# Two-layer gated cross-attention block on one core: weighted sums of three key blocks in a row, 12 probability buffers, and a new step for most other work

## What is computed

```python
x = x + tanh(g_xattn[0]) * attention(layernorm(x), ctx)        # 16 heads of 16 channels
x = x + tanh(g_ffn[0])   * ternary_linear(layernorm(x))        # scale: a maximum over all of x
x = x + tanh(g_xattn[1]) * depool(layernorm(x), ctx, lengths)
x = x + tanh(g_ffn[1])   * int8_linear(layernorm(x))
# attention, for each batch and head:
k = concat(ctx_k, k); v = concat(ctx_v, v)                      # 120 + 256 = 376 keys
out = softmax(q * scale @ k.T) @ v                              # then @ w_proj.T + b_proj
```

## Time and profile before

| | before |
|---|---|
| median of 3 runs | 1188.46 us (1187.54 to 1188.80) |
| profiled execution | 1188.27 us, span 1186.5 us |
| busy share of the span | PE 93%, DVE 79%, ACT 70%, POOL 59% |
| granted TensorE clock, mean | 0.97 of full speed |
| attention stage | about 65 to 967 us of the span |
| row stage | about 975 us to the end |

### The profile page before, as it was taken

The page is one execution under the profiler, slowest core; times in us unless marked ns, Lnnn a source line. Parts: engine busy times, 40 slices in busy tenths (PEclk is TensorE's granted clock), DMA queues, the critical chain, the costliest instruction groups (busy, mean ns, idle before and its releaser), DMA issues.

```text
span 1186.5 us, 33451 instructions
## 1 busy us (share of the span) xinstructions
PE 1106.6 (93%) x8458; PEld 679.4 (57%) x8458; DVE 935.8 (79%) x2328; ACT 833.3 (70%) x1730; POOL 699.4 (59%) x1259
## 2 busy tenths in 40 slices
PE   3599999999999999999999999999999968988885
PEld 3255555555555555555555555555555537767673
DVE  4867777777777777777777777777777736999997
ACT  2157777777777777777777777777777747878874
POOL 4545666655555556655566665666664217777776
PEclk9699999999999999999999999999999977999997
DMA  4333343333333333333333333333333101222222
GB/s 135 96 83 105 103 105 105 97 100 102 101 101 101 101 105 96 97 101 99 96 98 101 101 102 100 103 103 106 88 94 86 40 26 35 69 86 86 86 87 88
DMA packets 158680, 110.18 MB, mean 93 GB/s; under 512 B 17154, under 2 KB 154788, under 8 KB 158628
## 3 DMA queue, kind: packets, MB, share of 16 engines
q1 hardware_dynamic: 156900, 108.78, 33.9%
q10 hardware_dynamic: 1728, 0.79, 0.2%
HBM read 30.30 MB, written 16.29 MB: 39 GB/s over the span
## 4 chain that ended last, share of the span: by engine, by line
PE 78%; DVE 10%; issue 4%; POOL 4%; DMA 1%; ACT 1%; DVEq 1%; POOLq 0%; SPq 0%; ACTq 0%
PE pv_ps L622 18%; PE ms_ps L607 16%; PE st_ps L597 15%; PE misc L645 9%; PE misc L648 5%; PE misc L653 5%; PE aux L669 2%; PE misc L637 1%; PE aux L674 1%; PE aux L663 1%; DVE am L1176 1%; DVE xs L1165 1%; DVE v L1159 1%; POOL xs L1035 1%; PE st_ps L1104 1%
## 5 line engine op out<-in xcount | busy, mean ns | idle before, releaser
L790 DVE TENSOR_REDUCE neg<-ms_ps 128x1 f32<-128x376 f32 x1024 | 528.7, 544 | 185.8 <-PE ms_ps L607 173.9
L887 ACT ACTIVATE probs<-st_ps 128x512 f32<-128x512 f32 x768 | 449.7, 601 | 156.8 <-PE st_ps L597 83.3
L607 PE MATMUL ms_ps<-k,q 96*128 96x376 bf16 x1024 | 335.0, 328 | 7.1 <-DVE neg L790 6.6
L597 PE MATMUL st_ps<-q,k 99*128 99x256 bf16 x1536 | 295.6, 274 | 0.7 <-ACT probs L887 0.6
L622 PE MATMUL pv_ps<-probs,v 128*32 128x256 f32 (+1 forms) x3072 | 245.4, 391 | 0.5 <-ACT oT L903 0.2
L597 PEld LDWEIGHTS st_ps<-q,k 99*128 99x128 bf16 x1536 | 134.4, 98 | 90.9 <-ACT probs L887 29.1
L607 PEld LDWEIGHTS ms_ps<-k,q 96*128 96x128 bf16 x1024 | 98.7, 96 | 128.5 <-DVE neg L790 115.4
L645 PE MATMUL misc<-xnT,wqkvT 128*128 128x256 f32 x512 | 155.1, 387 | 2.3 <-ACT xnT L916 1.5
L622 PEld LDWEIGHTS pv_ps<-probs,v 128*32 128x32 f32 (+1 forms) x3072 | 60.5, 108 | 117.5 <-issue 87.9
L468 POOL TENSOR_SCALAR negp<-neg 128x16 bf16<-128x16 f32 x64 | 13.0, 204 | 175.4 <-DVE neg L790 175.0
L485 POOL TENSOR_SCALAR parts<-qk 128x632 bf16<-128x632 f32 x64 | 46.0, 719 | 99.9 <-ACT qk L953 99.7
(11 more groups left out here) (186 smaller groups left out, 1821.2 us busy)
## 6 DMA issues: line engine op xcount, KB each, us to landing
k<-parts SPq DMA_DIRECT2D x384, 94.0 KB, 2.7
q<-parts SPq DMA_DIRECT2D x384, 64.0 KB, 2.4
xs<-in_x SPq DMA_DIRECT2D x32, 256.0 KB, 2.8
out_dram<-xn SPq DMA_DIRECT2D x32, 256.0 KB, 2.2
cx<-in_ctx SPq DMA_DIRECT2D x32, 240.0 KB, 2.8
recurrence_input<-u_in SPq DMA_DIRECT2D x32, 120.0 KB, 1.9
plug<-plugs SPq DMA_DIRECT2D x32, 120.0 KB, 3.2
powers<-gath SPq DMA_DIRECT2D x32, 120.0 KB, 1.9
```

The source lines that it names most:

```text
L597: mm = pe.matmul(st_ps[u % SR][:, j * S:(j + 1) * S], k6[0:KM, r, h, k * P:(k + 1) * P], q6[0:KM, r, h, :], start=True, stop=True)
L607: pe.matmul(ms_ps[t][:, 0:KEYS], q6[0:KR, r, h % HU, t * P:(t + 1) * P], k6[0:KR, r, h % HU, 0:KEYS], start=True, stop=True).then_inc(s_ms, 1)
L790: dve.tensor_reduce(neg[:, m, t, h % HU:h % HU + 1], ms_ps[t][:, 0:KEYS], AX.X, ALU.max, negate=True).then_inc(s_red, 1)
L887: act.activation(probs[:, u % PR, :], st_ps[u % SR][:, :], ACT.Exp).then_inc(s_exp, 1)
```

## The change

- `PR` goes from 8 to 12 buffers `probs`. At steps 1, 7, 13 and 19 PE now calls `attend` three times in a row, for the three key blocks of one head group; no other step has one.
- `negT` has a half for each of `neg0` and `neg1`. ACT only copies; the DMAs of the maxima rows are started by SP, `neg1`'s first in the body and `neg0`'s between the load of `cx` and the stack of half 1.
- The jobs and what ACT and DVE do get new steps (table `AT`): PE's `k`, `proj` and `v` one step later, `xT` at step 1, `o0` at 9; ACT's `xn` at 12 and 14, `decay` at 12, `vcx` at 14, `neg0` at 20 (21 before), `xnT` at 0; DVE's `norm` at 4, 10, 16 and 22, `mn` at 7, `mx` at 8, `update` at 18, `gath` at 21, `aggr1` at 23; and the second score blocks of a step move from steps 1 and 3 to steps 2 and 4 of each six.

The diff, cut to its core:

```diff
-    PR = 8
+    PR = 12
-        negT = sb("negT", [3 * HU, S], BF16)
+        negT = sb("negT", [3 * HU, 2, S], BF16)
         JOBS = {
-            "xT": (0, 0, 1, 2), "q": (0, 2, 4, 2), "k": (0, 7, 4, 2), "proj": (0, 13, 4, -1), "v": (0, 19, 4, 1),
-            "kcT": (1, 2, 1, 2), "o3": (1, 4, 1, -1), "aT": (1, 6, 1, -1), "neg1": (1, 8, 1, 0), "o0": (1, 10, 1, 0),
+            "xT": (0, 1, 1, 2), "q": (0, 2, 4, 2), "k": (0, 8, 4, 2), "proj": (0, 14, 4, -1), "v": (0, 20, 4, 1),
+            "kcT": (1, 2, 1, 2), "o3": (1, 4, 1, -1), "aT": (1, 6, 1, -1), "neg1": (1, 8, 1, 0), "o0": (1, 9, 1, 0),
             "o1": (1, 16, 1, 0), "neg0": (1, 20, 1, 1), "o2": (1, 22, 1, 0),
         }
+        AT = {
+            "cxp": 0, "xnT": 0, "copy_o": 2, "kc": 4, "csq": 4, "q": 6, "aT": 6, "neg1": 8, "xn": 12, "k": 11, "decay": 12,
+            "vcx": 14, "neg0": 20, "v": 23,
+            "stats0": 1, "aggr0": 2, "norm": 4, "update": 18, "stats1": 19, "aggr1": 23, "mx": 8, "mn": 7, "gath": 21,
+        }
-            counts = [1, 2, 1, 2, 1, 1] * NG
+            counts = [1, 1, 2, 1, 2, 1] * NG
...
                 b, opp = i * 2 + par, 1 - par
+                if live(b):
+                    own_wait_taken(sp, b, "neg1")
+                    sp.dma_start(q6[KR:KM, 2 * par + 1, :, :], negT[:, 1, :]).then_inc(d_neg[2 * par + 1], 16)
...
                     sp.dma_start(cx[0:NP, opp, :], ctx_2048[b + 3]).then_inc(d_cx[opp], 16)
+                if live(b + 1):
+                    own_wait_taken(sp, b, "neg0")
+                    sp.dma_start(q6[KR:KM, 2 * opp, :, :], negT[:, 0, :]).then_inc(d_neg[2 * opp], 16)
                 if live(b + 2):
                     stack(b + 2, par, 1)
...
                     if u == 1 and live(b - 1):
-                        attend(b - 1, opp, NG * NKT - 1)
-                    elif u % 2 and u > 1 and live(b):
-                        attend(b, par, (u - 3) // 2)
+                        for k in range(NKT):
+                            attend(b - 1, opp, (NG - 1) * NKT + k)
+                    elif u % (2 * NKT) == 1 and u > 1 and live(b):
+                        for k in range(NKT):
+                            attend(b, par, (u // (2 * NKT) - 1) * NKT + k)
...
-                def neg_rows(B, pB, m, waits):
+                def neg_rows(B, iB, pB, m):
                     wait_full(act, b, f"neg{m}")
-                    if waits:
-                        act.wait_ge(d_neg[2 * par + 1 - m], i * 16 + 16)
-                    act.copy(negT[:, :], aux[:, :].bitcast(BF16)[0:3 * HU, 0:S]).then_inc(s_free[1], 1)
-                    own_wait_taken(act, b, f"neg{m}")
-                    act.dma_start(q6[KR:KM, 2 * pB + m, :, :], negT[:, :]).then_inc(d_neg[2 * pB + m], 16)
+                    if live(B - 1):
+                        act.wait_ge(d_neg[2 * (1 - pB) + m], (iB + (pB - 1) // 2) * 16 + 16)
+                    act.copy(negT[:, m, :], aux[:, :].bitcast(BF16)[0:3 * HU, 0:S]).then_inc(s_free[1], 1)
```

More of the change, by code:

```diff
@@ L812, in body @@
                     maxima([first])
-                    if u == 1 and live(b + 3):
+                    if u == AT["stats0"] and live(b + 3):
                         dve.wait_ge(d_x[opp], (i + (par + 3) // 2) * 16 + 16)
@@ L819, in body @@
                             dve.bn_stats(bn[:, t, :], xs[:, b + 3, t, :]).then_inc(s_stat0, 1)
-                    if u == 4 and live(b + 3):
+                    if u == AT["aggr0"] and live(b + 3):
                         own_wait(dve, s_stat0, (b + 3) * 4 + 2)
@@ L823, in body @@
                             dve.bn_aggr(mv0[:, t, :], bn[:, t, :]).then_inc(s_stat0, 1)
-                    if u == 5 and live(b - 1):
+                    if u == AT["norm"] and live(b - 1):
                         normalise(b - 1, 3)
-                    if u in (10, 16, 22) and live(b):
-                        normalise(b, (u - 10) // 6)
-                    if u == 17 and live(b - 1):
+                    if u > AT["norm"] and u % 6 == AT["norm"] % 6 and live(b):
+                        normalise(b, (u - AT["norm"]) // 6 - 1)
+                    if u == AT["update"] and live(b - 1):
                         wait_full(dve, b, "proj")
@@ L833, in body @@
                                                  xs[:, b - 1, :, :], ALU.mult, ALU.add).then_inc(s_free[0], 1)
-                    if u == 19 and live(b - 1):
+                    if u == AT["stats1"] and live(b - 1):
                         own_wait_taken(dve, b, "proj")
@@ L837, in body @@
                             dve.bn_stats(bn1[:, t, :], xs[:, b - 1, t, :]).then_inc(s_x1, 1)
-                    if u == 21 and live(b - 1):
+                    if u == AT["aggr1"] and live(b - 1):
                         own_wait(dve, s_x1, (b - 1) * 6 + 2)
@@ L843, in body @@
                             dve.bn_aggr(mvt[:, t, :], bn1[:, t, :]).then_inc(s_x1, 1)
-                    if u == 7 and live(b - 2):
+                    if u == AT["mx"] and live(b - 2):
                         dve.tensor_reduce(mx1[:, bass.ds((b - 2) * T, T)], xs[:, b - 2, :, :], AX.X, ALU.max).then_inc(s_x1, 1)
-                    if u == 13 and live(b - 2):
+                    if u == AT["mn"] and live(b - 2):
                         dve.tensor_reduce(mn1[:, bass.ds((b - 2) * T, T)], xs[:, b - 2, :, :], AX.X, ALU.min).then_inc(s_x1, 1)
-                    if isinstance(b, int) and b == LAST and u == 22:
+                    if isinstance(b, int) and b == LAST and u == HS - 1:
                         dve.tensor_reduce(mx1[:, bass.ds((b - 1) * T, T)], xs[:, b - 1, :, :], AX.X, ALU.max).then_inc(s_x1, 1)
                         dve.tensor_reduce(mn1[:, bass.ds((b - 1) * T, T)], xs[:, b - 1, :, :], AX.X, ALU.min).then_inc(s_x1, 1)
-                    if u == 23 and live(b):
+                    if u == AT["gath"] and live(b):
                         dve.wait_ge(s_dist, b + 1)
@@ L905, in body @@
                 for u in range(HS):
-                    if u == 0 and live(b + 2):
+                    if u == AT["cxp"] and live(b + 2):
                         act.wait_ge(d_cx[par], (i + 1) * 16 + 16)
@@ L925, in body @@
                         act.copy(qk[:, :, 2 * S:FC], aux[:, 0:2 * P].rearrange("p (m r) -> p m r", m=2)[:, :, 0:NP]).then_inc(s_free[1], 1)
-                    if u == 4 and live(b + 1):
+                    if u == AT["csq"] and live(b + 1):
                         act.wait_ge(d_cx[opp], (i + (par + 1) // 2) * 16 + 16)
@@ L930, in body @@
                         act.activation(cjunk[0:NP, :], cx[0:NP, opp, :], ACT.Square, accum_out=csq[0:NP, 0:1]).then_inc(s_csq, 1)
-                    if u == 6 and live(b + 2):
+                    if u == AT["q"] and live(b + 2):
                         wait_full(act, b, "q")
                         act.mul(qk[:, :, 0:S], misc[:, :].rearrange("p (m r) -> p m r", m=2), SCALE).then_inc(s_free[0], 1)
-                    if u == 7 and live(b - 1):
+                    if u == AT["aT"] and live(b - 1):
                         wait_full(act, b, "aT")
                         act.copy(attnT[:, :, :], aux[:, :].rearrange("p (k r) -> p k r", r=S)).then_inc(s_free[1], 1)
-                    if u == 8 and live(b):
-                        neg_rows(b, par, 1, True)
-                    if u == 10 and live(b + 3):
+                    if u == AT["neg1"] and live(b):
+                        neg_rows(b, i, par, 1)
+                    if u == AT["xn"] and live(b + 3):
                         B = b + 3
@@ L946, in body @@
                             wait_full(act, b - 1, "xT")
-                    if u in (10, 12) and live(b + 3):
-                        t = (u - 10) // 2
+                    if u in (AT["xn"], AT["xn"] + 2) and live(b + 3):
+                        t = (u - AT["xn"]) // 2
                         act.activation(xn[:, opp, t, :], xs[:, b + 3, t, :], ACT.Identity, bias=rn0[:, 3, t:t + 1],
                                        scale=rn0[:, 1, t:t + 1]).then_inc(s_xn, 1)
-                    if u == 11 and live(b + 2):
+                    if u == AT["k"] and live(b + 2):
                         wait_full(act, b, "k")
                         act.copy(qk[:, :, S:2 * S], misc[:, :].rearrange("p (m r) -> p m r", m=2)).then_inc(s_free[0], 1)
-                    if u == 15 and live(b - 1):
+                    if u == AT["decay"] and live(b - 1):
                         act.wait_ge(s_plug, b)
                         act.activation(gath[0:NP, opp, :], gath[0:NP, opp, :], ACT.Exp, scale=-DT).then_inc(s_decay, 1)
-                    if u == 17 and live(b + 1):
+                    if u == AT["vcx"] and live(b + 1):
                         if live(b - 1):
@@ L961, in body @@
                         act.copy(v[0:NP, opp, T, :, 0:D], cx[0:NP, opp, C:CC].rearrange("p (h d) -> p h d", d=D)).then_inc(s_vcx, 1)
-                    if u == 21 and live(b + 1):
-                        neg_rows(b + 1, opp, 0, live(b))
-                    if u == 23 and live(b + 1):
```

(3 more changed lines are left out.)

10 lines of the change are left out of this document (5 added, 5 removed).

## The result

The changed kernel takes 1168.04 us (median of 4 runs, 1165.75 to 1168.73) against 1188.34 us for the kernel before on the same chip: ratio 0.9825, 95% interval 0.9811 to 0.9839, so 20.3 us faster. The forecast was 1158 us in a range of 1142 to 1178: right in direction, inside the range, and 10 us too low. The profiled execution has a span of 1166.9 us, 19.6 less than before.

The account below looks back on a forecast made before the run. PE was taken to bound the attention stage at 28.3 us a batch; 28.3 − 1.45 + 0.45 = 27.3, so −1.0 over 30 batches, −30 us from 1188.3, gave 1158 us, range 1142 to 1178.

Parts of the forecast that it names:

- −8 × 0.18 = −1.45: Attends on PE: 12 entries and exits of the 32-column tiles become 4, saving 1.45 us a batch.
- Twelve buffers hide the exponentials' wait: Exponentials: with twelve buffers the needed attend stands at least four steps back, so no wait for groups; costed at nothing.
- Longer bursts: A group holds PE 1.62 us without new banks for DVE and ACT; hold-ups of 0.4 to 0.9 us, some 0.4 existing today.
- ACT's relief brings nothing: ACT no longer starts two DMAs of 1.04 us each; it has slack, so no gain itself.
- `neg1` through SP costs nothing: Rows of neg1 before step 12: land 3.0 us after the start, PE needs 3.3; cost 0, at worst 0.3.
- `neg0` through SP sets the period: Step 0: neg0 rows land 13.4 us after job k, PE comes 0.7 to 0.8 early; net +0.45 us a batch.
- 30 batches × the period: Whole kernel: −1.0 us a batch counted for 30 batches, −30 us, since the last ones have no q and k jobs.
- The whole gain arrives: Rival, 20%: the SP chain is hidden, −1.45 × 30 = −43.5, 1145 us.
- Weight loads stand exposed: Rival, 10%: loads of a group's 2nd and 3rd attend cost PE 0.9 us; −0.6 × 30, 1171 us.
- Bursts starve DVE: Rival, 10%: DVE idles 1.5 us in each of four groups and hold-ups double; 27.9 us a batch, 1176 us.
- the mode cost stays: Rival, 5%: the cost belongs to each attend's new accumulation, not the tile change; nothing gained, 1188 us.
- Slower: Rival, 8%: neg0 rows become the bound, 1.8 us late, neg1 late too (0.3); 28.7 us a batch, 1200 us.

Follow-up runs that it names:

- spread: The changed kernel with its attends single again, one to an odd step; 1196.3 us, ratio 1.0060 to the kernel before.
- pr8: The changed kernel with 8 probability buffers instead of 12; 1165.8 us, ratio 0.9808 to the kernel before.
- act_dma: The changed kernel with both maxima rows' DMAs started by ACT again instead of SP; 1167.0 us, ratio 0.9815 to the kernel before.
- gath23: The changed kernel with DVE's gath at step 23 instead of 21; 1164.2 us, ratio 0.9794 to the kernel before.
- before_group: The kernel before with only the attends grouped in threes, still 8 buffers, ACT's DMAs and old steps; 1224.4 us, ratio 1.0297 to the kernel before.
- cx_mid: The changed kernel with gath at 23 and SP loading cx inside the stack of half 0, then neg0, then powers; 1144.4 us, ratio 0.9631.
- gath1: The changed kernel with gath cut to one column of 256; 1163.6 us, ratio 0.9783 to the kernel before.
- act_gath23: The changed kernel with gath at 23 and both maxima rows' DMAs started by ACT; 1162.0 us, ratio 0.9787 to the kernel before.
- cx_small: act_gath23 with SP's cx load cut to 8 of 512 columns, so later batches use a stale context; 1143.4 us, ratio 0.9624.

## Why the prediction was right, and where it was off

- **PE bounds the stage, and a change of tile costs about 0.18 us.** Right in kind; `spread` and the change differ by 28 us. The term was mis-sized: "−8 × 0.18 = −1.45" is −1.8. The step that failed is "0.48 of streaming": I took the 0.24 us between the two sets of an attend for pure streaming and paid it six times in a group. In a run of three, 1.44 us less the 0.57 of the last attend leaves 0.87 for two attends, 0.435 each, or 0.22 a pass, as in a projection part. So the longer first pass and the exit belong to the change of tile too, and 0.45 us saved for two changes less is 0.225 each.
- **Twelve buffers hide the exponentials' wait.** Wrong reason: with eight, `exp(u)` waits at most for the first attend of a group, and ACT's `copy_o` of the same step waits for the whole group anyway; `pr8` loses nothing. Costed at nothing, rightly.
- **Longer bursts.** The place was right (step 23, behind `gath`), the size not: "about 0.4 at step 23" measured 0.68. I took `gath`'s 0.96 us as a duration. It depends on POOL, and at step 21 it starts near the beginning of a POOL operation: 1.28.
- **ACT's relief brings nothing.** Right: `act_dma` equals the change.
- **`neg1` through SP costs nothing.** Right; from 300 to 800 us PE's waits name `q<-negT` once, with 0.2 us.
- **`neg0` through SP sets the period.** Right in what the wait is, and nearly in size: SP started the DMA 10.9 us after the `k` copy (498.03 to 508.97) where the working gave 11.0. Wrong in the mechanism: I saw a chain of issues that ends with the rows' own DMA, and gave "`neg0` behind `cx` in one queue" as a second bound of the same length. It is that second one alone: the chain counts up to the issue of `cx`, and through ACT's queue, 0.2 us ahead of `cx`, the rows still come with the end of `cx`. The sign to look for was missed too: 0.4 to 0.5 us on `q<-negT` once a batch. In the change only 0.19 us of it show, since DVE's hold-up comes just before; `gath23` shows it whole, 0.75 us a batch.
- **The sum.** Forecast: −1.45 + 0.45 = −1.0. Measured: 28.34 to 27.47 = −0.87, of which −1.8 is the groups' and +0.9 the waits'. Gain and loss were both forecast too small, by 0.35 and 0.45; that the sum is off by 0.13 only is luck.
- **30 batches × the period.** From the first `xT` of the batch loop to the last, 29 periods, the trace gives 819.2 − 795.9 = 23.3 us. The start gives some back: that first `xT` stands at 73.5 us instead of 69.2. The eleven variants of the changed kernel have it at 70.3 to 73.1 us and `before_group`, with the old steps, at 69.2. So a part of the 4.3 us is scatter between executions; how much isn't settled.
- **Rivals.** "The whole gain arrives" was refused for a good reason (1145 us): it needed the SP order of `cx_mid`, which then took 1144.4, though by other sums: −1.8 for the groups and some 0.2 of waits left. "Weight loads stand exposed" fell: 24 loads are done within 1.02 us under 1.44 us of matmuls. The Trainium skill's sentence in "TensorE: Matmul & The Clock Gate", Part 3, that weight loads overlap running matmuls only in other row groups, disagrees with this trace. "Bursts starve DVE" and "the mode cost stays" fell. "Slower" didn't come for the change, but `before_group` shows its mechanism: rows that come late, at 29.42 us a batch. The rival's sum of 28.7 counts 1.8 us of lateness and leaves out the 0.3 that it names for `neg1`.
- **The clock.** It stayed at 1.00 as expected, but the reason given, that no hole is near a microsecond, wasn't needed: in `before_group` PE waits up to 1.4 us at a time, and the granted clock from 300 to 600 us is 1.00 as well.

## What to carry to other kernels

Instructions of one tile shape belong together: each change from 128-column to 32-column tiles and back cost 0.225 us here. But a burst on the bounding engine moves every deadline around it, and half the gain went to waits that stood in parallel; taking one away shows nothing until the other goes too, so look at the period and at which wait is left, not at the time alone. And order a DMA queue by who needs what first: here a small transfer with a deadline landed with the large one started just before or after it, whoever issued it.

## What the runs showed of the hardware

- DVE's `gath` operation, with two inputs in SBUF, stands still while a POOL operation with two inputs in SBUF that began before it runs. One column took 1.0 us, and ended 0.03 after POOL's end; with no POOL operation beside it, it took 0.14. 256 columns ended 0.28 after POOL's end (508.95 + 1.28 = 510.23, POOL 509.95). Over the whole change the operation's shortest case is 0.41 us, the last one, with POOL at rest, and its longest 1.48:

```profile
L869 DVE SCALAR_TENSOR_TENSOR gath<-plug x32: 407/1282/1475, 95.7 to 940.3; 120x256 f32<-120x256 f32 x32
```

  The Trainium skill, "SBUF — State Buffer", section "SBUF: two separate sides", says the same: a DVE instruction with two SBUF inputs and a GpSimd instruction, where the latter reads SBUF, exclude each other, and the later one blocks fully. The traces agree for a DVE operation that comes second: one column, 0.14 us of work, isn't done before the other's end. In the first instance of `gath1` it began 0.05 us before POOL's operation (92.66 and 92.71) and took 0.15.
- A 12 KB DMA on another queue than the 240 KB load beside it came no sooner for that. In `act_gath23` the 27 packets of the `neg0` rows start 2.2 to 2.8 us after the issue, and PE's step 0 3.2 us after it; in `cx_small`, with the load cut, they start 1.4 to 1.8 us after the issue, and PE doesn't wait. Whether the packets or the making of their descriptors stood in line was not tried.
